# Expert gates of a fused attention and mixture-of-experts block: spread over the channels by transfers through memory in fp32 instead of by matmuls in bf16, with a longer token pipeline

## The chip, the cores and the metric

The kernel runs on one core of one Trainium2 chip. The core has four compute engines that run side by side, each through its own instructions in order: PE (TensorE, matrix products), DVE (VectorE, elementwise work and reductions), ACT (ScalarE, functions of one input) and POOL (GpSimd). SP (SyncE) computes nothing: it issues transfers between the chip's memory (HBM) and the on-chip memory SBUF. POOL issues transfers as well. PE writes its results to PSUM, which has eight banks. Engines wait for each other with semaphores. The metric is the device time of one run in microseconds (us).

## The reference

The input x is 8 images of 64 channels and 96 by 96 pixels, in fp32. In short:

```python
x = x + attention(ln_c(x))        # two window attentions (4x4 windows, one of them shifted by 2), halves of the channels apart
t = to_tokens(x)                  # (8, 9216, 64)
t = t + ffn(ln_t(t))

def ffn(x, router_w, router_b, expert_w, expert_b):   # E = 8 experts, K = 2 chosen per token
    router_probs = softmax(x @ router_w + router_b)
    top_p, top_i = top_k(router_probs, 2)
    top_p = top_p / sum(top_p)
    expert_out = einsum("bnd,edc->bnec", x, expert_w) + expert_b
    gathered = take_along_axis(expert_out, top_i[..., None], axis=2)
    return einsum("bnk,bnkc->bnc", top_p, gathered)
```

The kernel computes all experts for each token: it multiplies the normalised token by the gate of the expert (zero for the six that were not chosen), multiplies that by the expert's matrix, and adds over the experts. For that, a gate, one number for each token and expert, must stand beside all 64 channels of its token.

## The kernel before, in words

An image is cut into 24 strips of 4 rows (384 pixels for each of 128 partitions: two halves of 64 channels), a strip into 3 units of 8 windows. Attention works on strips and units. The token part (feed-forward) works on tiles of two strips: 96 tiles of 768 tokens, the two strips on the two halves of the partitions.

The whole is one software pipeline, written out by hand. Time is cut into slots, one for each unit, so a strip has 3 slots and a tile has 6. The table `LAG` says how many slots after its first unit a step stands. In each slot every engine runs, in a fixed order, the steps that are due. `strip("x")` and `tile("x")` hold in the one slot in which that step is due; `in_tile("x")` gives the slot's number within the six. The program writes the first slots out, then loops over an image, then writes the rest out. The order on each engine is thus fixed, and an engine goes on only as semaphores allow.

What matters for the change, of one tile whose first unit is in slot 0:

- SP stores the attention result `fin` of each strip to the tensor `z` in HBM with 11 transfers (L401, `store_z`, lag 15). In slot 24 it waits until the stores of all strips that the tile needs have landed, and issues 7 loads of x and z (L433, `load_tile`). It also loads later strips (L371) and stores the result (L450).
- DVE adds x and the two z parts to `y` in slot 27 (L968 and L982, `tile_sum`). PE subtracts the mean of `y` in the same slot (L648), and the variance, the router's product and the logits follow in slots 28 to 30. `y` has two buffers.
- DVE finds the two best experts and their gates from slot 31 on, in 22 small steps of 48 values a partition (`gate_step_of`, L860 to L892). The last five of them split the gates into three bf16 parts.
- PE turns the parts to rows in slot 34 (L572), ACT copies them to `gateT` (L705), PE adds the experts' biases (L670, three bf16 products).
- In slots 35 to 38, for each of the 8 experts: PE spreads that expert's gate over 64 channels with one bf16 product into `bank_g` (L532, `spread_gate`). DVE multiplies it by the tokens (L917, `gate_product`, the tokens copied to both halves of the partitions in `yn_pair`). PE frees `bank_g` for the next expert only after that. After each second expert PE multiplies by their matrices (L543).
- In slot 39 DVE adds `y` and the experts' sum (L945), and SP stores it.
- POOL issues the small transfers that arrange keys and values for the attention (L479 `kx`, L490 `vx`, 8 and 16 a strip) and `yn_pair` (L500, 4 a tile), and adds two of the nine taps of a depthwise convolution (L509). DVE adds the others (L929).

## Time and profile before

| | |
|---|---|
| median of 3 runs | 3803.37 us (3798.1 to 3808.32) |
| the profiled execution, device time | 3802.88 us |
| its span, first to last instruction | 3801.0 us |
| busy PE, DVE, POOL, ACT | 86%, 84%, 77%, 58% of the span |
| granted TensorE clock, mean | 0.943 |
| share of time in which the 16 DMA engines are busy, 1000 to 1400 us | 0.29 |

Rows of the profile read so. In the chain of waits a row is a start, a length and what ran. "SPq" is SP's own queue of instructions, "PEld" PE's loading of weights. A row of waits names who waited, for whom, the total in us, how often, and the longest. A row of groups names line, engine, operation, tensors, shapes and the count, then busy us in total and mean ns of one, then the idle time in front of it. A row of the timeline is a start in us, a length in us, then what ran and how often. A row of windows gives, for a stretch, its length, the busy time of each engine with its number of instructions, the granted clock of TensorE (1.00 is 2.4 GHz, 0.5 is 1.2 GHz), the DMA engines' share and GB/s. Instructions that follow each other on DVE may overlap by about 0.09 us, so starts give the cost of one in a row better than lengths do.

### The profile page before, as it was taken

Reading aid. Unit: us, or ns where it says so; the run is one execution under the profiler, and the core shown is the slowest. Engines: PE = TensorE matmul, PEld = TensorE weight load, DVE = VectorE, ACT = ScalarE, POOL = GpSimd, SP = SyncE. Lnnn points to the kernel's source line nnn. Section 1 sums busy time; section 2 is a strip of 40 time slices with the busy share of each in tenths; the row PEclk is TensorE's granted clock in tenths of the full one; section 3 lists DMA queues with packets and bytes.
Section 4 is the critical chain, followed back from the end, with each engine's and each line's share of the span. In section 5 each row is a group of like instructions: output and inputs, shape, how many; then the busy total and the mean of one; then the engine's idle time right before and its main releaser. Section 6 shows DMA issues by size and latency. Waiting matters only on the chain.

```text
span 3801.0 us, 207759 instructions
## 1 busy us (share of the span) xinstructions
PE 3274.6 (86%) x83621; PEld 1990.9 (52%) x83621; DVE 3207.6 (84%) x7044; ACT 2223.4 (58%) x4516; POOL 2920.3 (77%) x5385
## 2 busy tenths in 40 slices
PE   3889898888888888888888988888888898889985
PEld 1655555555555555555555555555555555555541
DVE  2789988888888888988888888888888888999983
ACT  2666655665656656565566665666565665666641
POOL 3988878787878777878787877787787878888860
PEclk8999999999999999999999999999999999999985
DMA  1232323232323222323222232322232323233221
GB/s 32 59 81 73 82 70 82 70 82 68 83 70 80 71 76 76 78 75 78 72 74 78 74 78 72 80 75 78 69 81 69 82 71 82 73 84 79 76 65 39
DMA packets 307856, 279.35 MB, mean 73 GB/s; under 512 B 122368, under 2 KB 288304, under 8 KB 306864
## 3 DMA queue, kind: packets, MB, share of 16 engines
q1 hardware_dynamic: 140976, 152.09, 15.2%
q0 software_dynamic: 165888, 113.57, 12.0%
q8 instruction: 680, 11.14, 1.3%
q14 instruction: 312, 2.56, 0.2%
HBM read 95.33 MB, written 56.62 MB: 40 GB/s over the span
## 4 chain that ended last, share of the span: by engine, by line
PE 25%; SPq 22%; DVE 20%; issue 16%; DMA 10%; ACT 5%; DVEq 1%; POOL 1%; POOLq 0%; ACTq 0%
SPq L401 14%; SPq L433 7%; PE bank L629 6%; DMA z2t<-z 6%; DVE lepe L929 4%; DMA z<-fin 4%; PE bank L584 3%; PE bank L634 3%; PE bank L561 3%; DVE fin L989 3%; PE bank L656 3%; DVE gx L917 2%; PE bank L543 2%; DVE prob L949 2%; ACT row_inv L701 2%
## 5 line engine op out<-in xcount | busy, mean ns | idle before, releaser
L490 POOL DMA_DIRECT2D vx<-vt x3072 | 1555.3, 515 | 623.8 <-issue 487.2
L629 PEld LDWEIGHTS bank<-probT,vx 128*32 128x32 f32 x36864 | 827.9, 191 | 254.1 <-issue 250.4
L629 PE MATMUL bank<-probT,vx 128*32 128x16 f32 x36864 | 888.7, 235 | 25.2 <-issue 23.6
L479 POOL DMA_DIRECT2D kx<-k_sb x1536 | 737.8, 488 | 119.3 <-ACT k_sb L748 100.3
L561 PEld LDWEIGHTS bank<-kx,qx 32*32 32x32 f32 x36864 | 571.6, 109 | 330.6 <-issue 326.9
L561 PE MATMUL bank<-kx,qx 32*32 32x64 f32 x36864 | 673.8, 221 | 54.3 <-issue 46.1
L929 DVE SCALAR_TENSOR_TENSOR lepe<-vpad,lepe_sb,lepe 128x384 f32<-128x384 f32 x960 | 675.8, 704 | 0.0
L917 DVE TENSOR_TENSOR gx<-bank,yn_pair 128x384 f32<-128x384 f32 x768 | 424.2, 552 | 280.6 <-PE bank L532 277.6
L543 PE MATMUL bank<-gx,expert_sb 128*64 128x384 f32 x1536 | 343.1, 526 | 173.2 <-DVE gx L917 171.3
L725 ACT ACTIVATE prob<-prob 128x512 f32<-128x512 f32 x576 | 359.8, 625 | 199.3 <-DVE prob L949 189.9
L509 POOL TENSOR_TENSOR lepe_p<-lepe_p,tap_sb 128x384 f32<-128x384 f32 x384 | 424.7, 1106 | 27.5 <-issue 6.1
L937 DVE TENSOR_REDUCE row_max<-bank 128x32 f32<-128x512 f32 x576 | 393.4, 683 | 16.6 <-issue 10.1
L1004 DVE STREAM_TRANSPOSE probT<-prob 128x512 f32<-128x512 f32 x576 | 404.6, 702 | 0.0
L949 DVE TENSOR_TENSOR prob<-bank,row_max 128x512 f32<-128x512 f32 x576 | 393.5, 683 | 11.5 <-issue 7.5
L731 ACT ACTIVATE bank<-bias_tile 128x512 f32<-128x512 f32 x576 | 339.1, 589 | 0.0
L543 PEld LDWEIGHTS bank<-gx,expert_sb 128*64 128x64 f32 x1536 | 77.4, 137 | 405.8 <-DVE gx L917 405.8
L532 PE MATMUL bank<-gateT,expert_sel 128*128 128x384 bf16 x768 | 262.1, 341 | 9.4 <-DVE gx L917 9.0
L753 ACT ACTIVATE xs<-bank 128x384 f32<-128x384 f32 x192 | 94.1, 490 | 288.5 <-PE bank L642 288.5
L739 ACT ACTIVATE qx<-bank,const_sb 128x384 f32<-128x384 f32 x384 | 201.3, 576 | 103.5 <-PE bank L601 103.5
L500 POOL DMA_DIRECT2D yn_pair<-yn x384 | 199.0, 526 | 73.8 <-DVE yn L972 45.4
L763 ACT ACTIVATE tap_sb<-vpad,lepe_sb 128x384 f32<-128x384 f32 x384 | 234.1, 610 | 0.0
L532 PEld LDWEIGHTS bank<-gateT,expert_sel 128*128 128x128 bf16 x768 | 74.1, 96 | 238.1 <-issue 182.5
(101 smaller groups left out, 4803.6 us busy)
## 6 DMA issues: line engine op xcount, KB each, us to landing
vx<-vt POOLq DMA_DIRECT2D x3072, 12.0 KB, 1.9
kx<-k_sb POOLq DMA_DIRECT2D x1536, 24.0 KB
yn_pair<-yn POOLq DMA_DIRECT2D x384, 96.0 KB
z<-fin SPq DMA_DIRECT2D x1344, 24.0 KB
xs<-in_x SPq DMA_DIRECT2D x96, 192.0 KB
xt<-in_x SPq DMA_DIRECT2D x192, 96.0 KB
z0t<-z SPq DMA_DIRECT2D x192, 96.0 KB
out_y<-y_out SPq DMA_DIRECT2D x192, 96.0 KB, 2.2
```

Source lines behind the costliest of these rows:

```text
L401: sp.dma_start(z_cols[roll][im][:, a, b, q0:q1, :, here] .rearrange("b q y n -> q y (b n)"), fin[part:part + 2 * (q1 - q0), r % 2, :])\
L479: pool.dma_start(kx[to + m:to + C:4, r % 2, m, :], k_sb[at + m:at + C:4, r % 2, :])\
L490: pool.dma_start(vx[to:to + TOK, r % 2, g * 8 + x:g * 8 + 8:2, odd, :], vt[at:at + TOK, r % 2, x::2, :, :].rearrange("p h n k -> p h (n k)"))\
L509: G.tensor_tensor(lepe_p[:, kr % 2, :], lepe_p[:, kr % 2, :], tap_sb[:, j - 1, :], ALU.add).then_inc(pool_lepe_made, 1)
L543: last = MM(bank_f[half * C:(half + 1) * C, 0:SPX], expert_sb[:, e // 2, :], gx[:, (e - 1 + half) % 4, :], start=False, stop=(e == E - 1), ...
L561: last = MM(bank_s[r % 2][at, w * KEYS:(w + 1) * KEYS], qx[at, kr % 2, win, :, :].rearrange("p a i -> p (a i)"), kx[at, kr % 2, :, win * T ...
L629: last = MM(bank_o[32 * c:32 * c + 32, at * TOK:(at + 1) * TOK], vx[:, kr % 2, :, at % 2, at // 2 * 4 + c], probT[:, kr % 2, at, c * TOK:( ...
L917: V.tensor_tensor(gx[:, e % 4, :], bank_g[:, 0:SPX], yn_pair[:, r % 2, e % 2, :], ALU.mult)\
L929: V.scalar_tensor_tensor(acc, vrows(r, t // 3 - 1, t % 3 - 1), lepe_sb[:, t:t + 1], first if j == 0 else acc, ALU.mult, ALU.add).then_inc( ...
L937: V.tensor_reduce(row_max[:, r % 2, :], per_row(bank_s[r % 2][:, :]), AX.X, ALU.max).then_inc(max_made, 1)
L949: V.tensor_tensor(per_row(prob[:, r % 4, :]), per_row(bank_s[r % 2][:, :]), over_keys(row_max[:, r % 2, :]), ALU.subtract).then_inc(shifte ...
L1004: V.transpose(probT[:, kr % 2, j * UW:(j + 1) * UW, :].rearrange("p n k -> p (n k)"), prob[:, r % 4, :]).then_inc(probT_made, 1)
```

## The change

The gates stay in fp32, and the splitting into parts is gone (17 steps instead of 22). PE turns them to 16 rows (in `bank_g`, which is otherwise free now, so that the logits' turning moves there from `bank_o` too), ACT copies them to `gateT`, and SP stores them to a small tensor in HBM, `gate_rows` (one transfer of 16 rows of 384 values). Two slots later SP loads them back with four transfers, each of which reads 4 rows and writes them to 64 partitions: `gate_wide`, 128 partitions of 8 times 384 values, which has one buffer. The eight products on PE with `expert_sel` are gone. DVE multiplies two halves at once: four products of 768 values, both inputs in SBUF, instead of eight of 384 with one input in PSUM. The experts' biases are one fp32 product instead of three in bf16.

The steps of the token part stand further apart: the two additions for `y` in slots 28 and 29, PE's first step on it in slot 30, the gates from 36 on, their store in 39, their load in 41, the products in 44 to 46, the matrices in 45 to 47, the last addition in 47. `y` has four buffers, the other tensors two as before.

```diff
-    store_z=15, load_tile=24, tile_sum=27, tile_variance=28, router=29, logits=30, gates=31,
-    pair_yn=31, gap_exp=33, turn_gates=34, experts=35, tile_out=39)
+    store_z=15, load_tile=24, y_first=28, y_second=29, tile_sum=30, tile_variance=31, router=32, logits=33,
+    take_logits=34, gates=36, gap_exp=37, turn_gates=38, pair_yn=38, store_gates=39, spread_gates=41,
+    expert_bias=43, products=44, experts=45, tile_out=47)
-EXPERT_AT = {(0, 0): 0, (0, 1): 1, (1, 0): 2, (1, 1): 3, (2, 0): 4, (2, 1): 5, (3, 0): 6, (3, 1): 7}
+PAIRS = E // 2
+PRODUCT_AT = {(0, 1): 0, (1, 0): 1, (1, 1): 2, (2, 0): 3}
+EXPERT_AT = {(0, 0): 0, (1, 0): 1, (1, 1): 2, (2, 0): 3}
...
@@ SP
+                if ti := s.tile("store_gates"):
+                    k, r = ti
+                    wait_alone(sp, gateT_saved, k + 1)
+                    if s.later(r, 2):
+                        wait_alone(sp, gate_spread[r % 2], k // 2 * (GATE_DMAS * 16))
+                    sp.dma_start(gate_rows[r % 2], gateT[:, r % 2, :]).then_inc(gate_stored[r % 2], 16)
+                if ti := s.tile("spread_gates"):
+                    k, r = ti
+                    wait_alone(sp, gate_stored[r % 2], (k // 2 + 1) * 16)
+                    if s.later(r, 1):
+                        wait_alone(sp, gx_made, k * PAIRS)
+                    by_expert = gate_rows[r % 2].rearrange("(f p e) n -> e f p n", f=2, e=2)
+                    for odd in range(2):
+                        for half in range(2):
+                            sp.dma_start(gate_wide[odd * C:(odd + 1) * C, :, half, :],
+                                         by_expert[odd, half].unsqueeze(0).broadcast_to([C, PAIRS, SPX]))\
+                                .then_inc(gate_spread[r % 2], 16)
...
@@ PE
-                def spread_gate(k, r, e):
-                    if r * E + e >= 1:
-                        pe.wait_ge(gx_made, k * E + e)
-                    MM(bank_g[:, 0:SPX], expert_sel[:, e, :], gateT[:, r % 2, :], start=True, stop=True)\
-                        .then_inc(gate_spread, 1)
...
-                    for part in range(3):
-                        MM(bank_f[:, 0:SPX], ebias_part[:, part, :], gateT[:, r % 2, :], start=(part == 0), stop=(part == 2))
-                    spread_gate(k, r, 0)
+                    wait_alone(pe, gateT_saved, k + 1)
+                    MM(bank_f[:, 0:SPX], ebias_sb[:, :], gateT[:, r % 2, :], start=True, stop=True)
...
@@ DVE
-                    dve.wait_ge(gate_spread, k * E + (e + 1))
-                    if e == 0:
+                    if p == 0:
+                        dve.wait_ge(gate_spread[r % 2], (k // 2 + 1) * (GATE_DMAS * 16))
                         dve.wait_ge(yn_paired[r % 2], (k // 2 + 1) * 64)
-                    if r * E + e >= 4:
-                        dve.wait_ge(expert_made, k * (E // 2) + e // 2 - 1)
-                    V.tensor_tensor(gx[:, e % 4, :], bank_g[:, 0:SPX], yn_pair[:, r % 2, e % 2, :], ALU.mult)\
+                    if r * PAIRS + p >= 2:
+                        dve.wait_ge(expert_made, k * PAIRS + p - 1)
+                    V.tensor_tensor(gx[:, p % 2, :, :], gate_wide[:, p, :, :], yn_pair[:, r % 2, :, :], ALU.mult)\
                         .then_inc(gx_made, 1)
```

How the order moves on DVE, around the products of one slot. Before, these rows stand in the slot of the experts 2 and 3:

```order
L937 TENSOR_REDUCE row_max<-bank 128x32
L912 REGISTER_ALU
L917 TENSOR_TENSOR gx<-bank,yn_pair 128x384
L949 TENSOR_TENSOR prob<-bank,row_max 128x512
L986 REGISTER_ALU
L989 TENSOR_TENSOR fin<-att,lepe 128x24x4x4
L912 REGISTER_ALU
L917 TENSOR_TENSOR gx<-bank,yn_pair 128x384
L927 REGISTER_ALU
L929 SCALAR_TENSOR_TENSOR lepe<-vpad,lepe_sb,lepe 128x384
```

In the changed program the slot with two products reads so (a line number is that of the changed program: L907 is L937 before, L912 is L949, L887 is the product, L958 is `fin`, L899 is a tap):

```order
L907 TENSOR_REDUCE row_max<-bank 128x32
L912 TENSOR_TENSOR prob<-bank,row_max 128x512
L887 TENSOR_TENSOR gx<-gate_wide,yn_pair 128x768
L955 REGISTER_ALU
L958 TENSOR_TENSOR fin<-att,lepe 128x24x4x4
L886 REGISTER_ALU
L887 TENSOR_TENSOR gx<-gate_wide,yn_pair 128x768
L897 REGISTER_ALU
L899 SCALAR_TENSOR_TENSOR lepe<-vpad,lepe_sb,lepe 128x384
```

The first product of the slot now stands behind the two steps on the scores instead of between them, and each product has twice the width.

On DVE, around the addition for `y`. Before, both additions stand in one slot, close together and in front of `fin`:

```order
L968 TENSOR_TENSOR y<-xt,z0t 128x384
L856 REGISTER_ALU
L878 TENSOR_TENSOR gate_tmp<-gate_tmp,gate_vec 128x48
L981 REGISTER_ALU
L982 TENSOR_TENSOR y<-y,z2t 128x384
L986 REGISTER_ALU
L989 TENSOR_TENSOR fin<-att,lepe 128x24x4x4
```

In the changed program (L938 and L951 are the additions, L946 the copy of the logits, L980 the strip's normalisation):

```order
L938 TENSOR_TENSOR y<-xt,z0t 128x384
L946 COPY logits<-bank 128x48
L895 REGISTER_ALU
L899 SCALAR_TENSOR_TENSOR lepe<-vpad,lepe_sb,lepe_p 128x384
L971 REGISTER_ALU
L972 STREAM_TRANSPOSE probT<-prob 128x512
L897 ISA
L899 SCALAR_TENSOR_TENSOR lepe<-vpad,lepe_sb,lepe 128x384
L979 REGISTER_ALU
L980 TENSOR_TENSOR xs<-xs,rstd 128x384
```

The first addition is one slot later against the loads, the second one more, and no `fin` stands behind them in the slot of the first.

On SP, between the two groups of stores of a tile. Before:

```order
L401 DMA z<-fin 2x384
L450 DMA out_y<-y_out 64x384 x2
L401 DMA z<-fin 8x2x384 x7
```

In the changed program (L446 stores the gates, L455 spreads them, L464 stores the result):

```order
L397 DMA z<-fin 2x384
L446 DMA gate_rows<-gateT 16x384
L455 DMA gate_wide<-gate_rows 64x4x384 x4
L464 DMA out_y<-y_out 64x384 x2
L397 DMA z<-fin 8x2x384 x7
```

Five transfers more stand there for each tile, and the four that spread the gates wait for the one that stores them to land.

## Rows read from the trace of the kernel before

**Rows 1.** The chain that ended last, by line.

```profile
SPq L401 14%; SPq L433 7%; PE bank L629 6%; DMA z2t<-z 6%; DVE lepe L929 4%; DMA z<-fin 4%; PE bank L584 3%; PE bank L634 3%; PE bank L561 3%; DVE fin L989 3%; PE bank L656 3%; DVE gx L917 2%; PE bank L543 2%; DVE prob L949 2%; ACT row_inv L701 2%
```

**Rows 2.** The same chain in order of time, 1980 to 2025 us.

```profile
1982.67 0.48 DVE fin L989
...
1992.15 2.01 DMA z<-fin
...
1999.43 3.50 DMA z2t<-z
...
2020.54 0.48 DVE fin L989
```

**Rows 3.** Waits: who, for whom, us in total, times, longest.

```profile
DVE gx L917 <- PE bank L532: 277.6, 232, 5.0
DVE y L968 <- DMA z2t<-z: 113.2, 69, 4.9
PE bank L572 <- DVE gate_part L892: 114.2, 72, 3.3
PE bank L648 <- DVE y L982: 81.9, 53, 7.1
SPq L291 <- DVE fin L989: 875.8, 192, 11.3
```

**Rows 4.** The first addition for `y`: duration ns min/median/max, first and last start.

```profile
L968 DVE TENSOR_TENSOR y<-xt,z0t x96: 529/596/2168, 173.9 to 3754.4; 128x384 f32<-128x384 f32 x96
```

**Rows 5.** Windows of one tile's length: two of the four, and their mean.

```profile
1885.30:1923.00 37.70, 32.76 (x883) 20.22 (x878) 33.25 (x74) 23.44 (x49) 30.45 (x57) 1.00 0.29 76
...
1998.60:2036.50 37.90, 33.90 (x888) 20.96 (x885) 33.05 (x75) 23.16 (x47) 30.45 (x57) 0.95 0.30 78
sum 151.20, PE 132.14 PEld 81.40 DVE 133.27 ACT 93.00 POOL 121.80; mean PE 33.03 PEld 20.35 DVE 33.32 ACT 23.25 POOL 30.45
```

**Rows 6.** Groups of instructions, shapes apart.

```profile
L917 DVE TENSOR_TENSOR gx<-bank,yn_pair 128x384 f32<-128x384 f32 x768 | 424.2, 552 | 280.6 <-PE bank L532 277.6 <-issue 2.6
L949 DVE TENSOR_TENSOR prob<-bank,row_max 128x512 f32<-128x512 f32 x576 | 393.5, 683 | 11.5 <-issue 7.5
L532 PE MATMUL bank<-gateT,expert_sel 128*128 128x384 bf16 x768 | 262.1, 341 | 9.4 <-DVE gx L917 9.0
L1012 DVE TENSOR_TENSOR xs<-xs,rstd 128x384 f32<-128x384 f32 x192 | 106.3, 554 | 51.8 <-ACT rstd L712 51.8
L661 PE MATMUL bank<-yn,router_sb 128*16 128x384 f32 x192 | 78.6, 490 | 0.0
L670 PE MATMUL bank<-gateT,ebias_part 128*128 128x384 bf16 x288 | 65.4, 338 | 0.6 <-ACT gateT L705 0.6
L888 DVE CAST gate_part<-gate_tmp 128x48 bf16<-128x48 f32 x96 | 19.5, 203 | 3.3
```

**Rows 7.** Timeline of SP over one tile.

```profile
1892.79 9.18 SPq L401 DMA_DIRECT2D z<-fin  x11
1902.24 1.27 SPq L450 DMA_DIRECT2D out_y<-y_out  x2
1907.80 9.39 SPq L401 DMA_DIRECT2D z<-fin  x11
1919.01 0.59 SPq L433 DMA_DIRECT2D xt<-in_x  x1
...
1923.73 2.98 SPq L371 DMA_DIRECT2D xs<-in_x  x5
```

**Rows 8.** The queue of the transfers that SP issues: packets, MB, share.

```profile
q1 hardware_dynamic: 140976, 152.09, 15.2%
```

**Rows 9.** The taps on DVE: duration ns min/median/max, first and last start.

```profile
L929 DVE SCALAR_TENSOR_TENSOR lepe<-vpad,lepe_sb,lepe x960: 570/608/1877, 89.2 to 3704.6; 128x384 f32<-128x384 f32 x192
```

**Rows 10.** Timeline of DVE at 1984.5 us.

```profile
1984.45 1.57 DVE L929 SCALAR_TENSOR_TENSOR lepe<-vpad,lepe_sb,lepe 128x384 f32<-128x384 f32 x1
```

**Rows 11.** Timeline of POOL at the same time.

```profile
1984.58 2.35 POOL L509 TENSOR_TENSOR lepe_p<-lepe_p,tap_sb 128x384 f32<-128x384 f32 x2
```

More of the change, by code:

```diff
@@ L159, in _constants @@
         "mask_b": (p[:, None] // TOK % 4) == p[None, :4],
-        "expert_sel": np.stack([(p[:, None] % E == 2 * (i // 2) + p[None, :] // C) & (p[:, None] // E % 2 == i % 2)
-                                & (p[:, None] < 3 * GE) for i in range(E)], axis=1).reshape(128, E * 128),
         "rank": np.tile(E - np.arange(E), (128, 1)),
@@ L357, in _ @@
                         .then_inc(const_loaded, 16)
-                    for part in range(3):
-                        sp.dma_start(ebias_sb[part * GE + half * E:part * GE + (half + 1) * E, rows], expert_b)\
-                            .then_inc(const_loaded, 16)
+                    sp.dma_start(ebias_sb[half * E:(half + 1) * E, rows], expert_b).then_inc(const_loaded, 16)
             x_flat = x.rearrange("b c r w -> b c (r w)")
@@ L623, in slot @@
                             pe.wait_ge(log_made, k)
-                    if ti := s.tile("gates"):
-                        pe.wait_ge(logit_saved, ti[0] + 1)
                     for w in range(UW):
@@ L704, in slot @@
                     act.wait_ge(gateT_made, k + 1)
-                    S.activation(gateT[0:3 * GE, r % 2, :], bank_p[0][0:3 * GE, 0:SPX], ACT.Copy).then_inc(gateT_saved, 1)
+                    if s.later(r, 2):
+                        act.wait_ge(expert_made, (k - 1) * PAIRS)
+                    S.activation(gateT[:, r % 2, :], bank_g[0:GE, 0:SPX], ACT.Copy).then_inc(gateT_saved, 1)
                 if st := s.strip("variance"):
@@ L816, in _ @@
             dve.sem_inc(const_made, 1)
-            whole = ebias_sb[:, :]
-            for k in range(3):
-                chained(V.tensor_copy(ebias_part[:, k, :], whole))
-                if k < 2:
-                    chained(V.tensor_tensor(ebias_rest[:, k, :], whole, ebias_part[:, k, :], ALU.subtract))
-                    whole = ebias_rest[:, k, :]
-            dve.sem_inc(const_made, 1)
             GT = TBLK * 2
@@ L833, in wide, with gate_step_of @@
                 return vec.unsqueeze(2).broadcast_to([128, GT, E])
-            def by_block(flat):
-                return flat.rearrange("p (t a) -> p t a", a=GE)
             rank = const("rank").unsqueeze(1).broadcast_to([128, GT, E])
-            one1, one2, tmp, rest2, gates, left1, left2 = (gate_tmp[:, k, :] for k in range(7))
+            one1, one2, tmp, rest2, gates = (gate_tmp[:, k, :] for k in range(5))
             best1, best2, gap, vec, total, inv = (gate_vec[:, k, :] for k in range(6))
-            def part(k):
-                return gate_part[:, :, k, :]
-            GATE_SPLIT, GATE_STEPS = 12, 22
-            def gate_step_of(k, at):
+            GATE_SPLIT, GATE_STEPS = 12, 17
+            def gate_step_of(s, k, r, at):
                 if at == 0:
@@ L856, in gate_step_of @@
                     dve.wait_ge(gate_step, k * (GATE_STEPS - 2) + (at if at < GATE_SPLIT else at - 1))
+                if at == 14 and s.later(r, 1):
+                    dve.wait_ge(gateT_made, k)
                 best, src, hot = (best1, logits[:, :], one1) if at < 6 else (best2, rest2, one2)
@@ L880, in gate_step_of @@
                     done = V.tensor_tensor(gates, gates, one1, ALU.add)
-                elif at == 16:
+                else:
                     done = V.tensor_tensor(per_e(gates), per_e(gates), wide(inv), ALU.mult)
-                elif at == 17:
-                    done = V.tensor_copy(part(0), by_block(gates))
-                elif at == 18:
-                    done = V.tensor_tensor(by_block(left1), by_block(gates), part(0), ALU.subtract)
-                elif at == 19:
-                    done = V.tensor_copy(part(1), by_block(left1))
-                elif at == 20:
-                    done = V.tensor_tensor(by_block(left2), by_block(left1), part(1), ALU.subtract)
-                else:
-                    done = V.tensor_copy(part(2), by_block(left2))
@@ L893, in gate_step_of @@
-                done.then_inc(gap_made if at == 11 else gates_made if at == 21 else gate_step, 1)
+                done.then_inc(gap_made if at == 11 else gates_made if at == 16 else gate_step, 1)
             def slot(s):
-                ti = s.tile("gates")
                 working = s.in_tile("gates")
                 def gate_work(*steps):
-                    if working and working[2] < 3:
+                    if working and working[2] < 2:
                         for at in range(*steps[working[2]]):
-                            gate_step_of(working[0], at)
@@ L950, in slot @@
                                     over_keys(row_max[:, r % 2, :]), ALU.subtract).then_inc(shifted, 1)
-                gate_work((0, 0), (7, 8), (12, 13))
+                gate_work((1, 2), (12, 13))
+                gate_product(0)
+                if yt := s.tile("tile_out"):
+                    k, r = yt
+                    dve.wait_ge(expert_made, (k + 1) * PAIRS)
+                    if s.later(r, 2):
+                        dve.wait_ge(out_stored[r % 2], k // 2 * 32)
+                    V.tensor_tensor(y_out[:, r % 2, :], bank_f[:, 0:SPX], y[:, r % 4, :], ALU.add).then_inc(y_out_made, 1)
                 if st := s.strip("divide"):
```

129 lines of the change are left out of this document (53 added, 76 removed).

## The prediction

> **What bounds the kernel now.** I read the busy shares first: PE 86%, DVE 84%, POOL 77%, so no engine alone is the limit. The chain that ended last says what is. Its largest line is no compute at all: SP issuing the stores of `fin` (14%) and the loads of the tile (7%), with 6% for the landing of `z2t` and 4% for that of the stores [rows 1]. In order of time it is one loop a tile [rows 2]: `fin` is made at 1982.67, SP issues the 11 stores until 1992.15, they land 2.01 us later, 7 loads are issued and `z2t` lands at 1999.43 + 3.50 = 2002.93. Only then can DVE add `y`. The next `fin` of the chain starts at 2020.54, one tile (37.87 us) after the first. So 20.3 us of a tile are the way through memory, in which three slots stand, and the other 17.6 us are the work of the next three.
>
> The waits agree. DVE waited 277.6 us for the gate to be spread and 113.2 us for `z2t`, and PE 114.2 us for the parts of the gates and 81.9 us for `y` [rows 3]. A tile takes (3754.4 - 173.9) / 95 = 37.69 us [rows 4]. In four windows of a tile PE was busy 33.03, DVE 33.32, POOL 30.45 and ACT 23.25 us of 37.8 [rows 5]. DVE and PE each have some 4.5 us a tile of idle time, most of it in waits that the change touches: on DVE (277.6 + 113.2) / 96 = 4.07 us.
>
> **The change part by part, for one tile.**
>
> *DVE, products.* Eight of 552 ns go (4.42 us). For 768 columns the trace has no row. The same operation with both inputs in SBUF takes 554 ns at 384 columns and the step from 384 to 512 columns costs 683 - 552 = 131 ns, 1.02 ns a column [rows 6]. So 552 + 384 * 1.02 = 945 ns, four are 3.78 us. Neighbours on DVE overlap by 0.09 us, which four fewer instructions lose: 0.64 - 0.36 = 0.28 us gained. Bounds: 0.9 us each (nothing lost on overlap, gain 0.64) and twice 552 (no gain at all).
>
> *DVE, gate steps.* Five of about 0.20 us go, as L888 shows [rows 6]: 0.98 us. Bounds 0.6 (they overlap their neighbours) and 1.0. DVE stands at 33.32 - 0.28 - 0.98 = 32.06, with the small waits that stay (37.8 - 33.32 - 4.07 = 0.4 us) 32.5 us.
>
> *PE.* Eight spreads of 341 ns go, 2.7 us [rows 6]. Three bf16 products for the biases (3 * 338 ns, pipelined) become one in fp32, which is two passes of 490 ns like the router's [rows 6]: between 0.5 less and 0.2 more, taken as 0.1 more. The turnings stay at three. PE: 33.03 - 2.7 + 0.1 = 30.4 us. It waits no longer for `y` (made a slot earlier) nor for the gates (made in slots 36 and 37, turned in 38). The tile with clock 0.95 had 1.1 us more of PE than that with 1.00 [rows 5], and I expect fewer such stretches when PE's longest pause is gone. PE isn't the last, so I count nothing for it.
>
> *The wait for `z2t`.* The loads still start in slot 24, the first addition moves from 27 to 28. At 5.7 us a slot, that is 4 slots or 23 us for a way of 20.3 us, and it no longer sets the pace by itself. Cover gone (SP late by more than 2.5 us) brings part of the 1.2 us a tile back.
>
> *Waits added on DVE.* Product 2 waits for the first matrix product, product 3 for the second, the last addition for the fourth, each in the same slot on PE. They cost nothing as long as PE is ahead of DVE by about a microsecond, and by the sums above DVE is the slower of the two. From 0 to 1 us a tile; I take 0.3, so DVE needs 32.8 us.
>
> *POOL.* Same work, 30.45 us. `yn_pair` now stands behind the 16 `vx` transfers instead of in front, in every second strip, so the taps come 2 us later. The room before DVE needs them is two slots. No cost taken.
>
> *SP.* This is the engine that gets more work. Its tile before [rows 7]: stores 9.18 + 9.39, loads 1919.01 to 1923.73 = 4.72, `xs` 2.98, results 1.27, together 27.54 us; and 1.82 us in which it waits for the stores to land (1917.19 to 1919.01). That is 29.4 us, and the rest of the tile it waits for `fin` (875.8 us in all, 9.1 a tile [rows 3]). Added: one store like those of `fin` (9.18 / 11 = 0.83 us), four loads at 4.72 / 7 = 0.67 us (2.7 us), and the landing of the gates' store, between which and the spreading nothing else stands on SP: 1.8 us like the other. Together 5.3 us, so SP needs 34.7 us a tile, 32.9 if that landing falls into time in which it would wait anyway. For the issue of a transfer of 256 rows there is no row. It is bounded below by 0.5 us, and above by the time its data takes: the queue moved 152.09 MB in 15.2% of 16 engines' 3801 us, 263 GB/s, so 393 KB take 1.5 us [rows 8]. I take 0.67, since the loads of 64 rows there are nearest in kind. Behind a late SP stand the stores of `fin` and through them the loads of the next tile.
>
> *The transfers.* 4 * 393 KB = 1.57 MB a tile are 6.0 us of all 16 DMA engines: their share goes from 0.29 to about 0.29 + 6.0 / 34.4 = 0.46. From SP's slot 41 to the product late in slot 44 there are 3 slots, 17 us, against 2.7 of issue, 6.0 of data and 2 of landing. Hidden.
>
> *Sum.* The longest of the four decides: SP between 32.9 and 34.7, DVE 32.8, POOL and PE some 30.5. Two nearly full engines that hand work to each other do not reach the lower end, so I take 34.4 us a tile. Outside the 95 tiles are 3801.0 - 95 * 37.69 = 220.5 us. The first `y` comes a slot later (5 us). At the end the last tile passes store and spreading (about 14 us) but saves the passing to and fro of eight products: I take 10 us more. 220.5 + 15 + 95 * 34.4 = 3503.5, and with the 1.9 us between span (3801.0) and device time (3802.88) 3505 us. The median of the runs before, 3803.37, is the same as the profiled run's within 0.5 us, so nothing is corrected.
>
> **Rivals.**
> *B, the landing on SP is hidden and the issues are cheap.* Then DVE sets the pace at 32.8: 235.5 + 95 * 32.8 + 2 = 3354 us. For it: SP waits 9.1 us a tile today. Against it: those waits lie in front of each group of stores, not between store and spreading.
>
> *C, the spreading blocks SP.* If each of the four issues takes as long as its data (1.5 us instead of 0.67), SP needs 34.7 + 3.3 = 38 us; half of that is 36.4. So 235.5 + 95 * 37 + 2 = 3753, between 3695 and 3850. For it: SP's transfers go one after another, and landing takes longer behind others (3.50 us for `z2t` after six loads, 2.01 for the stores [rows 2]). The wait for `z2t` would then be back.
>
> *D, slower: the gates arrive late.* `gate_wide` has one buffer: SP may spread the next tile only after the fourth product, and DVE's first product waits for it. Issue 2.7, landing L, then two slots of products are one round: the tile takes at least (2.7 + L) * 1.5. It is slower than now once L is above 22.4 us, that is when the 1.57 MB move at under 70 GB/s instead of 263. For it: each of the four transfers reads the same few rows of HBM 64 times, which no row here does. Against it: it must be slower by a factor of three. At L = 24 it is 40 us a tile, 4038 us.
>
> *E, DVE and POOL hold each other up.* A tap on DVE took 1.57 us while POOL added its taps for 2.35 us [rows 10, 11]; the median is 0.608 [rows 9]. The products had one input in PSUM (mean 552 ns); now they read two in SBUF, like the tap. Two such POOL stretches fall in a tile, and if each holds a product for its whole 2.35 us, where the tap lost 1.57 - 0.608 = 0.96, that is 1.4 us more, DVE needs 32.8 + 2.8 = 35.6: 235.5 + 95 * 35.8 + 2 = 3639 us, still faster than now. What speaks against: the same stretch can hold only one instruction, and today it holds a tap or `y` as often. The Trainium skill, "SBUF — State Buffer", section "Who interferes with whom", states this rule: a DVE instruction with two SBUF inputs contends with a GpSimd instruction that reads SBUF, and the second to start is blocked until the first is done. By it the trace's 1.57 us agree, and it speaks against this change in that it gives four wide instructions to the lock that eight narrow ones did not need.
>
> **How the numbers follow.** Forecast 0.48, its own range 3440 to 3600. B 0.18, C 0.16, D 0.10, E 0.08. What a measurement can tell from no change is 0.3%, 11 us. Faster: 0.48 + 0.18 + 0.08 and 0.07 of C, 0.81. The same: 0.03 of C. Slower: D and 0.06 of C, 0.16. Predicted is 3505. The range goes from 3330 (two thirds of B above it) to 3810: left out are 0.06 below, and D and 0.04 of C above.
>
> **What would show it.** Right: DVE no longer waits for PE at the product nor for `z2t`; the chain has no landing of `z2t`; the product takes 0.93 to 0.97 us; SP's wait for `fin` falls from 9.1 to about 2 us a tile; the first `y` comes every 34.4 us; DMA share 0.46; granted clock above 0.95. Wrong: SP's wait for `fin` at zero with issues over 1 us (C); DVE waiting at the product for the transfer (D); products with a mean over 1.2 us (E); SP waiting much and DVE busy over 95% (B).

## The result, and the profile after

The changed kernel takes 3738.6 us (median of 4 runs, 3730.37 to 3753.5), the kernel before beside it 3800.73: a ratio of 0.983, 95% interval 0.981 to 0.986. It is faster by 1.7%. Forecast were 3505 us, 7.8% faster; the time lies within the range given, but the gain is a fifth of what was worked out.

The profiled execution took 3730.37 us. The first addition for `y`, as in [rows 4]:

```profile
L938 DVE TENSOR_TENSOR y<-xt,z0t x96: 546/552/1594, 173.7 to 3672.3; 128x384 f32<-128x384 f32 x96
```

A tile takes (3672.3 - 173.7) / 95 = 36.83 us, where 34.4 were forecast and 37.69 stood before. The time outside the tiles is 3728.5 - 95 * 36.83 = 229.6 us (forecast 235.5). So the whole miss, 95 * 2.4 = 231 us, lies in the length of a tile.

The waits that the change was about, as in [rows 3] (who, for whom, us in total, times, longest):

```profile
DVE gx L887 <- PE bank L549: 62.1, 57, 3.2
DVE gx L887 <- DMA gate_wide<-gate_rows: 50.2, 13, 9.3
DVE y L938 <- DMA z2t<-z: 11.7, 9, 3.3
SPq L289 <- DVE fin L958: 216.5, 87, 10.1
SPq L289 <- DMA gate_rows<-gateT: 193.1, 96, 5.8
```

The two waits of DVE that were to go have shrunk: 277.6 us for PE became 62.1, and 113.2 for `z2t` became 11.7. In their place stand others, and two of them have no partner to be waited for:

```profile
PE bank L628 <- issue: 144.0, 107, 5.4
PE bank L564 <- issue: 111.1, 57, 6.8
DVE att L925 <- ACT row_inv L692: 154.3, 73, 6.1
```

L628 and L564 are the small attention products (L629 and L561 in the kernel before, with 23.6 and 46.1 us there). "Issue" says that PE stood still although nothing it waits for in the profile was missing. DVE waited 15.1 us for `row_inv` before. That this wait follows from PE's pauses, one engine on, is read from its size in the runs below (43.4 us where the pauses are short). The groups, as in [rows 6], and the queues, as in [rows 8]:

```profile
L887 DVE TENSOR_TENSOR gx<-gate_wide,yn_pair 128x768 f32<-128x768 f32 x384 | 397.4, 1036 | 112.9 <-PE bank L549 62.1 <-DMA gate_wide<-gate_rows 50.2
L665 PE MATMUL bank<-gateT,ebias_sb 16*128 16x384 f32 x192 | 94.5, 573 | 1.5 <-DVE y_out L921 1.5
```

```profile
q1 hardware_dynamic: 248432, 304.94, 36.0%
q8 instruction: 671, 10.99, 1.3%
```

Queue q8 carries instructions: 671 blocks of 16 KB, 680 before the change. That is one block each 5.6 us. That queue has not grown. But what it has to share the DMA engines with has.

How such a pause looks. PE at 2669 to 2680 us:

```profile
2669.19 1.53 PE L628 MATMUL bank<-probT,vx 128*32 128x16 f32 x64
2677.56 1.77 PE L564 MATMUL bank<-kx,qx 32*32 32x64 f32 x57 [6.84 <-issue]
```

SP issued the gates' four transfers just as it began:

```profile
2669.06 2.67 SPq L455 DMA_DIRECT2D gate_wide<-gate_rows  x4
```

The DMA queues' share from 2662 to 2670 us, and then from 2670 to 2678 us:

```profile
q1 hardware_dynamic: 130, 0.12, 6.2%
q8 instruction: 1, 0.02, 1.0%
```

```profile
q1 hardware_dynamic: 982, 1.43, 87.0%
q8 instruction: 2, 0.03, 1.8%
```

For eight microseconds the gates fill the DMA engines, and PE gets no products done for 6.8 of them. This is the longest pause of all, and a special one: it stands where the loop over an image turns back to its start (PE's branch is at 2670.2 us). An ordinary one stands in the middle of a batch of 64 products, here after 53 of them, and the gates' transfers went out from 1880.05 us on:

```profile
1883.74 1.33 PE L628 MATMUL bank<-probT,vx 128*32 128x16 f32 x53
1890.47 0.45 PE L628 MATMUL bank<-probT,vx 128*32 128x16 f32 x11 [5.41 <-issue]
```

The records of the trace show all such pauses. Between 300 and 3600 us there are 91 pauses of PE over 1 us that are put to issue, 245.7 us together. Six of them (26.2 us) stand at a turn of the loop. All 91 end 1.14 to 2.2 us after one of the 16 KB blocks of q8 has landed. The stretches of 1.15 to 2.2 us behind all 671 blocks make up 19% of the span, so chance would put one pause in five there, not all. 87 of the 91 begin between 3.6 us before and 12.6 us after the first of a tile's four spreading transfers is issued. That is 16.2 us of 36.8, so chance would put fewer than half there. Before the change there are 20 of these pauses, 35.0 us together.

Two more counts speak of their cause. 77 of the 91 stand between two products of the same line, and in front of 80 there is no semaphore at all that PE would wait for. So the transfers of `kx` and `vx`, which PE also reads here and which share the same DMA engines, are not what it waits for. And if one counts PE's products and weight loads from one pause to the next, 80 of the 90 distances are a multiple of 256 (to within one); the other ten have an end within 8 us behind a turn of the loop. The 671 blocks against the 169,257 instructions that the profile has of PE are 252 to a block. So q8 brings PE's instructions, and a pause stands where a new block of them begins. The blocks come shortly before they are needed: behind the 80 pauses without a semaphore, each of the next five blocks lands 114 to 152 instructions (medians) before PE reaches it, and fewer than 218 in nine of ten cases. At PE's mean pace, 169,257 instructions in 3728.5 us, 130 instructions are an estimated 3 us. A burst of 8 us can use that up.

This gives theory T: the gates' 1.57 MB, sent in one burst, hold up the blocks of instructions that PE needs next. The Trainium skill, "Runtime: NRT & Kernel Launch", section "Instruction fetch mechanics", says that an engine's instructions come in 16 KiB blocks of 256 over a DMA queue of its own, and that the cost of crossing a block is "mostly hidden". The size agrees with the trace (10.99 MB in 671 blocks); so do the distances of 256. Hidden it is for the most part in the kernel before (35.0 us of such pauses), and no longer here.

The rivals: theory S, SP has too much to do (the chain that ended last still runs through its stores and loads, 13% L397, 4% L429); theory E, POOL and DVE hold each other up.

### The profile page after: what moved, and what is told of

Same layout as the page of the kernel before. It is cut to its first block, busy times and chain, and to the rows that moved or that the text cites. A ratio compares the mean times of both kernels' runs of the same rounds, so it can differ in the third digit from the quotient of the medians.

```text
span 3728.5 us, 203806 instructions
## 1 busy us (share of the span) xinstructions
PE 3199.5 (86%) x82757; PEld 1956.7 (52%) x82757; DVE 3190.4 (86%) x6174; ACT 2233.5 (60%) x4514; POOL 2942.7 (79%) x5385
## 3 DMA queue, kind: packets, MB, share of 16 engines
q8 instruction: 671, 10.99, 1.3%
## 4 chain that ended last, share of the span: by engine, by line
PE 36%; SPq 23%; issue 15%; DVE 14%; DMA 5%; ACT 3%; POOL 2%; DVEq 0%; ACTq 0%; POOLq 0%
SPq L397 13%; PE bank L628 8%; PE bank L564 7%; DVE lepe L899 4%; SPq L429 4%; PE bank L549 3%; PE bank L641 3%; PE bank L584 2%; SPq L455 2%; DVE gx L887 2%; PE bank L633 2%; DMA gate_rows<-gateT 2%; DVE row_max L907 2%; DMA z<-fin 2%; PE bank L653 2%
## 5 line engine op out<-in xcount | busy, mean ns | idle before, releaser
L628 PEld LDWEIGHTS bank<-probT,vx 128*32 128x32 f32 x36864 | 824.6, 189 | 464.5 <-issue 452.8
L628 PE MATMUL bank<-probT,vx 128*32 128x16 f32 x36864 | 886.3, 234 | 159.2 <-issue 144.0
L564 PEld LDWEIGHTS bank<-kx,qx 32*32 32x32 f32 x36864 | 584.9, 110 | 443.6 <-issue 441.3
L564 PE MATMUL bank<-kx,qx 32*32 32x64 f32 x36864 | 689.3, 223 | 133.3 <-issue 111.1
L899 DVE SCALAR_TENSOR_TENSOR lepe<-vpad,lepe_sb,lepe 128x384 f32<-128x384 f32 x960 | 673.5, 702 | 0.8 <-issue 0.8
L718 ACT ACTIVATE prob<-prob 128x512 f32<-128x512 f32 x576 | 367.4, 638 | 288.1 <-DVE prob L912 285.0
L887 DVE TENSOR_TENSOR gx<-gate_wide,yn_pair 128x768 f32<-128x768 f32 x384 | 397.4, 1036 | 112.9 <-PE bank L549 62.1
L523 POOL TENSOR_TENSOR lepe_p<-lepe_p,tap_sb 128x384 f32<-128x384 f32 x384 | 434.9, 1133 | 32.7 <-issue 11.3
L912 DVE TENSOR_TENSOR prob<-bank,row_max 128x512 f32<-128x512 f32 x576 | 398.4, 692 | 16.7
L907 DVE TENSOR_REDUCE row_max<-bank 128x32 f32<-128x512 f32 x576 | 393.8, 684 | 20.9 <-issue 14.4
L641 PE MATMUL bank<-xs,const_sb 128*128 128x384 f32 x384 | 201.0, 610 | 63.4 <-ACT qx L732 53.2
L703 ACT ACTIVATE rstd<-bank,const_sb 128x384 f32<-128x384 f32 x192 | 112.3, 585 | 219.0 <-PE bank L584 218.8
L925 DVE TENSOR_TENSOR att<-bank,row_inv 128x384 f32<-128x384 f32 x192 | 105.9, 552 | 154.5 <-ACT row_inv L692 154.3
```

Source lines behind the costliest of these rows:

```text
L523: G.tensor_tensor(lepe_p[:, kr % 2, :], lepe_p[:, kr % 2, :], tap_sb[:, j - 1, :], ALU.add).then_inc(pool_lepe_made, 1)
L564: last = MM(bank_s[r % 2][at, w * KEYS:(w + 1) * KEYS], qx[at, kr % 2, win, :, :].rearrange("p a i -> p (a i)"), kx[at, kr % 2, :, win * T ...
L628: last = MM(bank_o[32 * c:32 * c + 32, at * TOK:(at + 1) * TOK], vx[:, kr % 2, :, at % 2, at // 2 * 4 + c], probT[:, kr % 2, at, c * TOK:( ...
L887: V.tensor_tensor(gx[:, p % 2, :, :], gate_wide[:, p, :, :], yn_pair[:, r % 2, :, :], ALU.mult)\
L899: V.scalar_tensor_tensor(acc, vrows(r, t // 3 - 1, t % 3 - 1), lepe_sb[:, t:t + 1], first if j == 0 else acc, ALU.mult, ALU.add).then_inc( ...
L907: V.tensor_reduce(row_max[:, r % 2, :], per_row(bank_s[r % 2][:, :]), AX.X, ALU.max).then_inc(max_made, 1)
```

## The experiments

Each is compared with the kernel before on the same chip. That kernel took 3800.7 to 3809.2 us (medians) beside them, so a difference of 10 us between two experiments says nothing. "The changed kernel" is the one of the result. "Pauses over 1 us" are counted as above, between 300 and 3600 us.

**A quarter of the data (theory T against S).** The four transfers stay, each brings the gates of one pair of experts only; all products read these.

```diff
-sp.dma_start(gate_wide[odd * C:(odd + 1) * C, :, half, :],
-             by_expert[odd, half].unsqueeze(0).broadcast_to([C, PAIRS, SPX]))
+sp.dma_start(gate_wide[odd * C:(odd + 1) * C, 0, half, :],
+             by_expert[odd, half, 0].unsqueeze(0).broadcast_to([C, SPX]))
```

> The changed kernel, but each of the four spreading transfers of a tile moves only the first pair of experts (96 KB instead of 384 KB), and all four products use it: the gates of the other pairs are left out of the result. Instructions, waits and number of transfers are as in the changed kernel. Theory T (PE's own instruction blocks of 16 KB come late behind the 1.57 MB of gates): PE's pauses put down to issue at L628 and L564 fall from 255 us to under 90, a tile takes 34.4 to 35 us instead of 36.8, 3500 to 3570 us in all. Theory S (SP is full: same number of issues, same landing of the gates' store): 3720 to 3740, no change. Theory L (POOL's additions hold DVE's products): no change either, since the products are the same.

Measured: 3496.7 us, ratio 0.920 (0.916 to 0.924). The pauses:

```profile
PE bank L628 <- issue: 60.6, 101, 1.7
PE bank L564 <- issue: 43.1, 30, 5.5
```

This is the forecast's time within 9 us, at 34.62 us a tile, with all the instructions, waits and issues of the changed kernel. The amount of data by itself is worth as much as the forecast missed. The longest pause at L628 fell from 5.4 to 1.7 us. The pauses over 1 us are 17 instead of 91, 39.6 us instead of 245.7: 206 of the 242 us between the two. The granted clock rose from 0.923 to 0.962.

With the pauses gone another limit shows, the one that the sum had named. 55% of the chain that ended last is SP's issuing (23% in the changed kernel), SP waits only 89.5 us for `fin` (0.9 a tile), and the wait for `z2t` is back:

```profile
DVE y L938 <- DMA z2t<-z: 104.6, 51, 8.7
```

**POOL writes instead of adding (theory E).** POOL's two additions of taps are replaced by writing a constant, so it reads no SBUF there; these taps are missing from the sum.

```diff
-G.tensor_tensor(lepe_p[:, kr % 2, :], lepe_p[:, kr % 2, :], tap_sb[:, j - 1, :], ALU.add)
+G.memset(pool_out[:, :], 0.0)
```

> The changed kernel, but POOL's two additions of a strip (two inputs read from SBUF, 1.13 us each) are writes of a constant to a tensor of its own, about as long; the two taps are left out of the result. Theory L: the products' mean falls from 1036 to 950 ns and the small gate steps at L849 and L851 from 440 and 817 to 210 ns, DVE busy from 3190 to 3060-3100 us, and as DVE sets part of the pace the time to 3640-3690 us. Theory T: DVE gets faster all the same but waits for PE instead, 3710 to 3740 us.

Measured: 3724.9 us, ratio 0.978 (0.975 to 0.982), 14 us below the changed kernel's, which is little more than the scatter. DVE's busy time fell by 298 us, from 3190.4 to 2892.4, so the lock is real and large. The time hardly moved: DVE then waited for `row_inv` for 284.6 us instead of 154.3, and PE's pauses stayed (132.2 and 135.1 us). Theory E names a true cost that lay beside the limit.

**Paced transfers, on ACT's queue.** ACT issues the store of the gates, and then the four transfers one by one, half a slot apart, in slots 41 and 42. Nothing is left out.

```diff
+SPREAD_AT = {(0, 0): 0, (0, 1): 1, (1, 0): 2, (1, 1): 3}     # (slot, place in the slot): which of the four
...
+    odd, half = divmod(SPREAD_AT[(at, part)], 2)
+    S.dma_start(gate_wide[odd * C:(odd + 1) * C, :, half, :], ...)
```

> The changed kernel, but ACT issues the gates' store and the four spreading transfers, and these one by one, half a slot apart (slots 41 and 42), instead of all in one. Theory T: at most one such transfer (1.5 us of data) stands in front of an instruction block, so PE's pauses at L628 and L564 fall from 255 us to 100-150, and the time to 3580-3660 us. Theory S: SP is rid of 5.3 us a tile, 3580-3660 us too but with PE's pauses as long as before; the pauses tell. If neither: 3720-3760.

Measured: 3595.1 us, ratio 0.945 (0.942 to 0.949), 144 us faster than the changed kernel with the same data. PE's pauses were 103.8 us (89) and 101.0 us (74, longest 7.0). But two things were changed at once: the pace, and the queue, since SP no longer issues them. The next one takes them apart.

**All at once, on ACT's queue (theory S).** The same, all four transfers in slot 41 one after another.

```diff
-sp.dma_start(gate_wide[...])      # four of them, in SP's slot 41
+S.dma_start(gate_wide[...])       # four of them, in ACT's slot 41
```

> The changed kernel, with the store of the gates and the four spreading transfers issued by ACT instead of SP, all four at once as on SP. Theory T (the gates' 1.57 MB, sent at once, hold up the blocks of instructions that PE needs next): the data and its burst are the same, so PE's pauses put to issue stay near those of the changed kernel (144 us at L628 and 111 us at L564 there) and the time stays near it, 3680 to 3740. Theory S (SP is too full, and the paced version of 3595 us won only because its transfers left SP): the time is that of the paced version, 3580 to 3620, with SP waiting some 520 us for fin.

Measured: 3746.5 us, ratio 0.985 (0.981 to 0.988): as slow as the changed kernel, though SP is relieved:

```profile
SPq L289 <- DVE fin L958: 638.3, 174, 10.6
PE bank L546 <- issue: 143.2, 66, 8.0
PE bank L610 <- issue: 141.5, 106, 5.2
```

SP waits 638.3 us for `fin` instead of 216.5, and nobody gains. PE's pauses are near those of the changed kernel (141.5 and 143.2 against 144.0 and 111.1). Theory S falls as the cause of the miss, and what the paced version won, it won by the pace and not by the queue.

**The wider spacing alone.** The kernel before, with only the two additions for `y` in slots 28 and 29, the steps behind them three slots later, and `y` in four buffers. Gates and products are as before.

```diff
-    tile_sum=27, tile_variance=28, router=29, logits=30, gates=31, ... experts=35, tile_out=39)
+    y_first=28, y_second=29, tile_sum=30, tile_variance=31, router=32, logits=33, gates=34, ... experts=38, tile_out=42)
```

> The kernel before with one part of the change alone: y added in slots 28 and 29 in four buffers, every later token step three slots later, the gates still spread by PE in bf16. The reading of the chain (the way through memory of 20.3 us in three slots sets half of the tile): the wait for z2t goes, a tile takes 36.5 to 37 us instead of 37.7, 3690 to 3740 us. Rival: DVE and PE pass the products to and fro as before and fill the time, 3780 to 3810 us.

Measured: 3728.0 us, ratio 0.980 (0.976 to 0.983), 36.75 us a tile. No wait for `z2t` is left, that for the spread of the gates stays (274.8 us). So the spacing by itself gives what the whole change gives (the 11 us between them are within the scatter), and the gates by way of memory give nothing on top of it as they are sent there.

**The data without the change.** To the kernel before, four transfers of 384 KB a tile are added, of the same shape, from x into a tensor that no one reads, all in slot 35. PE's program is the same as before.

```diff
+for odd in range(2):
+    for half in range(2):
+        sp.dma_start(wide[odd * C:(odd + 1) * C, :, half, :],
+                     by_expert[odd, half].unsqueeze(0).broadcast_to([C, 4, SPX]))
```

> The kernel before, and beside it four transfers of 384 KB a tile, shaped like the spreading of the gates, from x into a tensor that nothing reads, issued by SP in slot 35. Nothing waits for them but the same transfers of the next tile. Theory T: PE's pauses put to issue rise from about 70 us to 200 or more although PE's program is unchanged, and the kernel is slower, 3880 to 4000. Theory S: it is slower only by what the small version costs. Theory N (data alone never costs, the changed kernel loses on its own waits): 3800 to 3830.

Measured: 4243.7 us, ratio 1.114 (1.109 to 1.118). Slower by 435 us, through transfers that nothing waits for. I had expected 3880 to 4000; the direction was theory T's, the size was beyond it. The longest pause is longer than any in the changed kernel. It stands at a turn of the loop, too (PE's branch is at 2036.3 us), and the longest elsewhere is 5.5 us, as in the changed kernel:

```profile
2036.76 0.48 PE L674 MATMUL bank<-yn,router_sb 128*16 128x384 f32 x1
2047.05 1.93 PE L574 MATMUL bank<-kx,qx 32*32 32x64 f32 x64 [9.80 <-issue]
```

```profile
2031.90 2.69 SPq L453 DMA_DIRECT2D wide<-in_x  x4
```

DVE stood still at the same time, also put to issue (the idle time in front of the row is in brackets):

```profile
2041.97 0.69 DVE L950 TENSOR_REDUCE row_max<-bank 128x32 f32<-128x512 f32 x1 [6.32 <-issue]
```

The burst falls here into the slots in which PE spreads gate by gate and DVE multiplies, and DVE's wait for that grew:

```profile
DVE gx L930 <- PE bank L545: 663.5, 340, 6.6
```

PE's pauses over 1 us are 82, 275.6 us together, against 20 and 35.0 us in the kernel before, and all 82 end 1.2 to 2.1 us after a block of instructions has landed. They are 241 of the 435 us. The rest is not taken apart: DVE's longer wait for the spread and the granted clock of 0.891 (0.943 before) go with them.

**The same issues, hardly any data.** As above, with 96 values a partition (24 KB) in each of the four.

```diff
-by_expert[odd, half].unsqueeze(0).broadcast_to([C, 4, SPX])
+by_expert[odd, half, 0, 0:96].unsqueeze(0).broadcast_to([C, 96])
```

> The same as the kernel with dummy traffic, but each of the four transfers carries 96 values a partition (24 KB) instead of 4 times 384 (384 KB). Issues on SP are the same in number. Theory T: no more pauses of PE than before, and a time of 3800 to 3850, from SP's four issues (2.7 us a tile, partly on the way through memory). Theory S: as slow as the version with the full traffic.

Measured: 3804.1 us, ratio 1.000 (0.998 to 1.002, 10 runs). Four more issues a tile on SP cost nothing, so the 435 us of the version above are its data.

**The same data, one transfer a slot.** As the version with all the traffic, in slots 35 to 38.

```diff
-if ti := s.tile("extra"):         # all four in slot 35
+if ti := s.in_tile("extra"):      # the at-th of four in slot 35 + at
```

> The kernel before with the same dummy traffic (four transfers of 384 KB a tile that nobody reads), but one in each of the slots 35 to 38 instead of all four in slot 35. Theory T (a burst holds up the blocks of instructions that PE is about to need): PE's pauses put to issue fall well below those of the version with all four at once (4244 us), and the time is 3850 to 4000. Rival V (it is the amount of data on the engines that costs, however it is spread): 4200 to 4280. Rival W (traffic while the products are passed to and fro is what costs, since every pause of PE there is a pause of DVE): also near 4240, with pauses at L545 and L556 as long as before.

Measured: 3989.9 us, ratio 1.049 (1.046 to 1.052). Set apart the same data costs 186 us instead of 435. PE's pauses over 1 us fell from 275.6 to 144.9 us. Rivals V and W, both near 4240, fall as the whole story. But not all is the burst: the pauses are still 110 us more than the 35.0 us of the kernel before, and it is still 5% slower. They are shorter and as many (81 against 82), and 70 of the 80 distances between them are again multiples of 256, so they are of the same kind: a single transfer of 384 KB is enough to make a block late. The wait for the spread gates (475.7 us, 294.7 in the version with little data) grew with them. How the 186 us divide between the two, no run separates.

**Eight transfers, pair by pair.** From the paced version: one pair of experts a slot in slots 41 to 44, in two transfers half a slot apart, and each product waits for its own pair only. Nothing is left out.

```diff
-gate_spread = sems("gate_spread")                       # one for all four, per parity of the tile
+gate_spread = [sem(f"gate_spread{p}") for p in range(PAIRS)]
...
+if s.later(r, 1):
+    wait_alone(act, gx_made, (k - 1) * PAIRS + p + 1)    # product p of the last tile is done
+S.dma_start(gate_wide[odd * C:(odd + 1) * C, p, :, :], by_pair[p, odd].unsqueeze(0).broadcast_to([C, 2, SPX]))
...
+dve.wait_ge(gate_spread[p], (k + 1) * 32)
```

> The paced version (3595 us), with eight transfers of 192 KB instead of four of 384 KB, one pair of experts a slot in slots 41 to 44, half a slot apart, each product waiting for its own pair only. Theory T: shorter bursts hold the blocks of instructions up less, PE's pauses put to issue fall from 104 and 101 us to 60 to 80 each, and the time is 3540 to 3580. Rival P (pacing over two slots took all that bursts cost, and what is left is the sum of the data): 3585 to 3605, same pauses. If ACT's four further issues a tile matter, it is slower than 3605.

Measured: 3481.3 us, ratio 0.913 (0.910 to 0.917). This beats both kernels: 8.7% under the kernel before, and the 1.57 MB a tile are all there. Three things differ from the paced version at once: the data stand over four slots instead of two, each product waits for its own pair only, and the same data took less of the DMA engines' time (5.6 us a tile instead of 7.6). Which of them won the 114 us, no run separates. It came out below the 3540 to 3580 that I had given it.

```profile
PE bank L610 <- issue: 63.9, 69, 2.4
PE bank L546 <- issue: 59.2, 56, 5.4
DVE gx L892 <- PE bank L531: 28.5, 22, 2.8
DVE gx L892 <- DMA gate_wide<-gate_rows: 11.2, 10, 2.6
```

```profile
q1 hardware_dynamic: 140912, 151.56, 17.2%
q10 hardware_dynamic: 113664, 153.41, 15.3%
```

A tile takes 34.54 us, and the granted clock is 0.957. The pauses (63.9 and 59.2 us) are about half of those of the changed kernel and near those with a quarter of the data (60.6 and 43.1). Those over 1 us are 46, 89.3 us together.

**The lock again, with the pauses gone.** The version pair by pair, with POOL writing a constant instead of adding its taps, which are missing from the sum.

```diff
-G.tensor_tensor(lepe_p[:, kr % 2, :], lepe_p[:, kr % 2, :], tap_sb[:, j - 1, :], ALU.add)
+G.memset(pool_out[:, :], 0.0)
```

> The version with eight transfers, pair by pair (3481 us), and POOL's additions of two taps replaced by writing a constant, so that POOL reads no SBUF there (the two taps are left out of the sum). With bursts gone DVE is busy 91% of the span. Theory E now (with the late blocks gone the lock between POOL and DVE is what sets the pace): DVE's busy time falls by some 290 us as it did in the changed kernel, and now most of it shows in the time, 3250 to 3350. Rival X (PE, POOL and the passing from engine to engine set the pace as well): less than a third of it shows, 3400 to 3470.

Measured: 3461.0 us, ratio 0.909 (0.907 to 0.911), 20 us less than pair by pair, at the edge of what the runs can tell apart. DVE's busy time fell from 3168.8 to 2887.4 us, and 7% of that shows. Rival X holds. PE is busy 90% of this span and POOL 85%, so there is no longer one engine whose relief shows, and the lock is a small cost here too.

## Why the prediction was wrong in size

*The step that failed* is "The transfers": "3 slots, 17 us, against 2.7 of issue, 6.0 of data and 2 of landing. Hidden." For the one who waits for the gates it was right: DVE waited 50.2 us in all for them, 13 times. But I asked only who waits for this transfer, and not what else uses the DMA engines in these 8 us. PE's instructions do. The shown cost is 3738.6 - 3496.7 = 242 us between all the data and a quarter of it, and 3738.6 - 3481.3 = 257 us between a burst and the same data in eight pieces, each as large as the miss of 234 us. PE's pauses over 1 us account for 206 of the 242 and for 156 of the 257. The sum had no term for it.

*Its size.* Also the data took longer than I estimated: queue q1 went from 15.2% of 3801 to 36.0% of 3728.5 us, that is 578 to 1342 us, 7.96 us a tile instead of 6.0. The share of the DMA engines was 0.52 instead of 0.46 in the middle of the run.

*SP.* The terms were right: 2.67 us for the four issues (2.7 forecast), 2.0 us a tile for the landing of the gates' store (1.8), a wait for `fin` of 216.5 / 96 = 2.3 us (about 2). Only the store's issue took 0.33 instead of 0.83 us. That the longest of the four sums decides did not hold for SP in the changed kernel: with (638.3 - 216.5) / 96 = 4.4 us a tile more room on SP the time stays the same (all at once on ACT's queue). Rival C falls with it; its issue time of 1.5 us did not come (median 0.62). The chain through SP's stores and loads stands in the profile all the same, but beside the late blocks it is not the one that counts. With a quarter of the data it is: SP's sum of 32.9 to 34.7 us stands against 34.62 measured, and 55% of the chain is SP's.

*DVE, products.* 1036 ns in the mean instead of 945. The shortest is 944 and the median 949, so the estimate for one undisturbed was right to 1%; the rest is POOL. The first row is DVE, the second POOL, at the same time, as in [rows 10, 11]:

```profile
1981.13 2.49 DVE L887 TENSOR_TENSOR gx<-gate_wide,yn_pair 128x768 f32<-128x768 f32 x1
...
1981.76 2.72 POOL L523 TENSOR_TENSOR lepe_p<-lepe_p,tap_sb 128x384 f32<-128x384 f32 x2
```

*DVE, gate steps.* The five gone were worth 0.98 us a tile, as said. But the seventeen steps that stay took 468.0 us instead of 404.3, 0.66 us a tile more, since other and more of them now fall beside POOL's additions (L878 and L880, 688 and 590 ns before, came free of them and take 208):

```profile
L849 DVE TENSOR_TENSOR gate_tmp<-gate_tmp,gate_vec 128x48 f32<-128x48 f32 x192 | 84.5, 440 | 3.8 <-issue 3.6
L851 DVE SCALAR_TENSOR_TENSOR gate_tmp<-gate_tmp,logits 128x48 f32<-128x48 f32 x96 | 78.4, 817 | 3.3
```

These two took 188 and 205 ns before, and take 202 and 208 where POOL only writes. So DVE was busy 32.6 us a tile (1000 to 3400 us) instead of 32.06. That a gain in one's own steps is lost by moving them beside another engine's was not in the sum. Neither mattered: without the lock the changed kernel is 14 us faster. Rival E named the right lock and the wrong price, 134 us (and its sum goes by 35.8 us a tile, where its terms add up to 35.6); "the same stretch can hold only one instruction" was the better argument.

*PE.* Forecast 30.4 us a tile; from 1000 to 3400 us it is 2111.4 us in 65.2 tiles, 32.4, and in the version pair by pair 31.6. Of the miss 0.2 us is the bias product (94.5 us in all against 65.4 before, 0.3 us a tile more where I took 0.1). I had expected the clock above 0.95 "when PE's longest pause is gone". It is 0.923, since PE has new and longer pauses, and it follows them: 0.962 with a quarter of the data, 0.957 pair by pair, 0.891 with the dummy traffic. How much of the time is the pause and how much the lower clock behind it, no run separates.

*Waits added on DVE.* 62.1 us at the product and 26.6 us at the last addition are 0.9 us a tile where I took 0.3; they come with PE's pauses and are 28.5 and 31.8 us pair by pair. POOL's later taps cost DVE 20.1 us instead of 14.7, as good as nothing, as said. Rival D's wait for the gates came to 50.2 us in 96 tiles, far from a bound.

*The wait for `z2t` and the spacing.* Right for the changed kernel: 113.2 us became 11.7, and the spacing alone gives 2.0%. But it was the long tile that hid it. At 34.62 us a tile with SP as full as here (a quarter of the data) it is 104.6 us, so at the forecast's own pace the cover of 2.5 us that the prediction gave it was used up. *The way out and in* was right within 6 us.

*The sum* of 34.4 us a tile comes out once the failed term is gone: 34.62 with a quarter of the data, 34.54 pair by pair. The first is the sum's own case, with SP at the limit. The second is luck: there SP has lost the five transfers that made up its sum, PE has 65% of the chain that ended last, and the same length comes of another limit. That two errors of DVE and PE (0.5 and 1.2 us a tile more) leave no trace in it shows how loose the allowance between the busiest engine and the tile's length was.

*Open:* the trace shows when a block of instructions lands and how long it moves (1.18 us in the mean, 1.14 before), not when it was asked for (only how far ahead of its use it lands). That PE's pauses stand where a new block begins is seen in the trace, and that the amount and the pace of other data make them is shown by the runs. That a block stands behind the gates' packets follows from both and is not seen itself. Open is also how the cost divides between the pauses, the lower clock behind them and the waits of the other engines.

## What to carry to other kernels

A transfer is hidden only if those who share its way are hidden too: beside the wait for its own data, count the microseconds in which it fills the DMA engines, and set against them the blocks of instructions of an engine that works in many small instructions (PE with some 860 products a tile). Waits put to "issue" that come in step with a large transfer are the sign. Count PE's instructions between such pauses, too: multiples of 256 gave the cause away here. The remedy was not less data but smaller pieces, set a half slot apart and each waited for by itself: 257 us here, of which the pace alone gave 144 to 151.

## What of the hardware was not expected

Data that nobody waits for slowed a kernel by 11%, with pauses of PE of up to 9.8 us and of DVE of 6.3 us at the same time, both at a turn of the loop, and of PE of up to 5.5 us elsewhere. In eight transfers of two rows each the same 1.57 MB took less of the DMA engines' time than in four of four rows: q10 15.3% of 3492.6 us, 5.6 us a tile, where the paced four took 20.2% of 3590.7 us, 7.6 us. Why is not known. PE's instructions arrive less than one block of 256 ahead of their use, some 3 us by the estimate above. And issuing from ACT's queue costs 0.59 us, on SP 0.62 (medians), and ACT, busy 65% of the span there, had room for it.
